# A vision block on one core: experts of the second image in swapped pairs, one write for the gates, and a new order on every engine

## What is computed

```python
# stage 1: gated 3x3 convolution (t = unfolded 3x3 patches, 576 values per pixel)
h1 = relu(t @ W1 + b1)
s = sigmoid(h1 @ W2 + b2)
h = (t * s) @ W3 + b3                      # 64 channels again; a class token is put in front
# stage 2: on n = layernorm(h)
a = n + linear_attention(rmsnorm(n, w_norm1)) @ w_out + b_out   # 8 heads, sums of k*v over all tokens of an image
h = h + a + rmsnorm(a, w_norm2)
# stage 3: on f = layernorm(h)
p = softmax(relu(f @ router_w1 + router_b1) @ router_w2 + router_b2)    # 6 experts
top_w, top_i = top_k(p, 2); g = softmax(top_w)
h = h + sum of g[k] * expert[top_i[k]](f)   # an expert is 64 -> 64 -> 64 -> 64 with relu; all six are computed
```

## Time and profile before

| | us |
|---|---|
| median of 3 runs | 2604.82 (2600.67 to 2604.88) |
| the profiled execution | 2603.84 |
| its span, first to last instruction | 2602.1 |
| TensorE busy | 2135.0 (82%) |
| VectorE busy | 1350.6 (52%) |
| ScalarE busy | 1103.6 (42%) |
| GpSimd busy | 511.4 (20%) |
| mean granted TensorE clock | 0.906 |

### The profile page before, as it was taken

The page is one execution under the profiler, slowest core; times in us unless marked ns, Lnnn a source line. Parts: engine busy times, 40 slices in busy tenths (PEclk is TensorE's granted clock), DMA queues, the critical chain, the costliest instruction groups (busy, mean ns, idle before and its releaser), DMA issues. The chain is left out here.

```text
span 2602.1 us, 36855 instructions
## 1 busy us (share of the span) xinstructions
PE 2135.0 (82%) x12353; PEld 921.4 (35%) x12353; DVE 1350.6 (52%) x3631; ACT 1103.6 (42%) x2213; POOL 511.4 (20%) x346
## 2 busy tenths in 40 slices
PE   7888878888878888888888888888888888876665
PEld 2333433333333333333334333333333333333322
DVE  4454646454545555564646464646464645544442
ACT  3443434444444444343534444444444444433233
POOL 1112212121221212122212121212121212121110
PEclk9998989899999989899989998999899999977777
DMA  2112222313131312222222222232313131211122
GB/s 106 61 61 63 63 71 53 84 46 91 46 91 46 88 49 80 57 69 68 69 68 67 71 66 71 57 81 56 81 46 91 46 91 46 51 43 43 44 48 58
DMA packets 41339, 168.30 MB, mean 65 GB/s; under 512 B 6048, under 2 KB 19264, under 8 KB 33984
## 3 DMA queue, kind: packets, MB, share of 16 engines
q1 hardware_dynamic: 41152, 165.95, 23.6%
HBM read 151.87 MB, written 14.05 MB: 64 GB/s over the span
## 5 line engine op out<-in xcount | busy, mean ns | idle before, releaser
L1243 DVE TENSOR_TENSOR gh<-f,gate_sp 128x448 f32<-128x448 f32 (+1 forms) x342 | 199.8, 612 | 436.5 <-issue 360.9
L682 ACT ACTIVATE th<-ps,b_half 128x448 f32<-128x448 f32 x504 | 294.8, 630 | 171.8 <-PE ps L354 106.4
L810 ACT ACTIVATE f<-ps,packed 128x448 f32<-128x448 f32 (+1 forms) x342 | 201.1, 630 | 371.9 <-DVE gh L1243 371.2
L920 DVE SCALAR_TENSOR_TENSOR gated<-th,x_tile 128x448 f32<-128x448 f32 x504 | 301.0, 617 | 16.3 <-PE ps L370 7.9
L388 PE MATMUL ps<-packed,rx_c 112*128 112x112 f32 (+1 forms) x225 | 56.7, 407 | 303.7 <-DVE rx_c L930 303.7
L856 POOL TENSOR_TENSOR rstd_u<-var_u,exponent 112x8 f32<-112x8 f32 (+1 forms) x57 | 92.3, 1619 | 1003.2 <-DVE var_u L946 1003.2
L326 PE MATMUL ps<-x_tile,packed 128*64 128x448 f32 x896 | 256.5, 693 | 2.0 <-DMA x_tile<-x_rows 2.0
L354 PE MATMUL ps<-h,packed 64*128 64x448 f32 x896 | 229.1, 588 | 9.8 <-ACT h L674 6.9
L370 PE MATMUL ps<-gated,w_half 128*64 128x448 f32 x896 | 203.7, 557 | 34.0 <-DVE gated L920 34.0
L856 POOL TENSOR_TENSOR rms_b<-ms_b,exponent 112x8 f32<-112x8 f32 (+1 forms) x57 | 107.3, 1882 | 591.2 <-DVE ms_b L1102 591.2
L610 PE MATMUL ps<-gh,packed 128*64 128x448 f32 (+1 forms) x684 | 216.7, 731 | 5.3 <-DVE gh L1243 5.3
(11 more groups left out here) (140 smaller groups left out, 3344.1 us busy)
## 6 DMA issues: line engine op xcount, KB each, us to landing
gate_sp<-gates_d SPq DMA_DIRECT2D x112, 672.0 KB, 7.0
x_tile<-x_rows SPq DMA_DIRECT2D x56, 696.0 KB, 5.2
x_tile<-x_rows SPq DMA_DIRECT2D x56, 580.0 KB, 3.8
out<-out_t SPq DMA_DIRECT2D x56, 224.0 KB, 8.1
gates_d<-gates_c SPq DMA_DIRECT2D x224, 5.2 KB
packed<-pack SPq DMA_DIRECT2D x1, 690.0 KB, 9.8
packed<-pack SPq DMA_DIRECT2D x1, 448.0 KB, 6.5
packed<-pack SPq DMA_DIRECT2D x1, 430.0 KB, 3.6
```

The source lines that it names most:

```text
L682: act.activation(th[(u + s) % 4][:, :], bank(S0 + u % 2), ACT.Tanh, bias=b2_half[:, m:m + 1], scale=0.5).then_inc(th_set, 1)
L810: act.activation(f2[j % 4][:, 0:n], bank(S0 + j % 2, n), ACT.Relu, bias=cst("eb2")[:, j:j + 1]).then_inc(f2_set, 1)
L920: dve.scalar_tensor_tensor(as_rows(gated[u % 4][:, :]), as_rows(th[(u + s) % 4][:, :]), 1.0, x_view(s, u), ALU.add, ALU.mult).then_inc(gat ...
L1243: dve.tensor_tensor(gh[j % 4][:, 0:n], f2[j % 4][:, 0:n], gate_sp[:, j, 0:n], ALU.mult).then_inc(gh_set, 1)
```

## The change

Image 1's experts are numbered with neighbours exchanged (1, 0, 3, 2, 5, 4) in the tables `rw2`, `order` and `eb3`. Its gates then come out of `gates_c` in an order in which even rows belong to the upper half and odd rows to the lower half for both images, so one write carries all 12 rows, and each read takes every second row. `gate_hidden` takes its slot accordingly. The order of the calls is new on every engine, and SyncE's list is longer by four steps.

```diff
-LAST_STEP = 70
+LAST_STEP = 74
@@ save_gates, spread_gates (SyncE)
-                for img in range(2):
-                    for low in range(2):
-                        top = (low + img) % 2
-                        sp.dma_start(gates_d[f % 2][top * E + img:top * E + E:2, 0:nt * tw],
-                                     gates_c[img * E + low:img * E + E:2, 0:nt * tw]).then_inc(gate_saved, 16)
+                sp.dma_start(gates_d[f % 2][:, 0:nt * tw], gates_c[:, 0:nt * tw]).then_inc(gate_saved, 16)
...
-                sp.wait_ge(gate_saved, 64 * f)
+                sp.wait_ge(gate_saved, 16 * f)
...
-                    rows = gates_d[f % 2][top * E:top * E + E, 0:n]
+                    rows = gates_d[f % 2][top:2 * E:2, 0:n]
@@ order on SyncE
-                if 1 <= step - 13 <= CLS_T: store_out(step - 13)
-                if 3 <= step + 1 <= BLOCKS: load_x(step + 1)
-                if 1 <= step - 10 <= CLS_T: save_gates(step - 10); spread_gates(step - 10)
+                if 3 <= step - 4 <= BLOCKS: load_x(step - 4)
+                if 1 <= step - 17 <= CLS_T: store_out(step - 17)
+                if 1 <= step - 14 <= CLS_T: spread_gates(step - 14)
+                if 1 <= step - 13 <= CLS_T: save_gates(step - 13)
@@ gate_hidden (VectorE)
-                dve.tensor_tensor(gh[j % 4][:, 0:n], f2[j % 4][:, 0:n], gate_sp[:, j, 0:n],
+                dve.tensor_tensor(gh[j % 4][:, 0:n], f2[j % 4][:, 0:n], gate_sp[:, j % 2 * (E // 2) + j // 2, 0:n],
@@ tables
+    swapped = [e + 1 - 2 * (e % 2) for e in range(E)]
+    for img, experts in enumerate((range(E), swapped)):
+        pack[img * E:img * E + E, eb3_at + 64 * img:eb3_at + 64 * img + 64] = eb3[list(experts)]
+        pack[RH * img:RH * img + RH, rw2_at + E * img:rw2_at + E * img + E] = a["L0_ffn_router_w2"][:, list(experts)]
+        pack[2 * RH, rw2_at + E * img:rw2_at + E * img + E] = a["L0_ffn_router_b2"][list(experts)]
...
+    put("order", np.tile(np.concatenate([first, first[swapped]]), (P, NT)))
```

More of the change, by code:

```diff
@@ L636, in _ @@
-                if 1 <= step - 1 <= BLOCKS: w3(step - 1, 4)
-                if 1 <= step - 9 <= CLS_T: spread_b(step - 9)
-                if 1 <= step - 10 <= CLS_T: gates_channels(step - 10); expert_h1(step - 10, 0)
+                if 1 <= step - 10 <= CLS_T: expert_h1(step - 10, 1); expert_h2(step - 10, 0)
+                if 1 <= step - 9 <= CLS_T: center_b(step - 9)
+                if 1 <= step - 10 <= CLS_T: expert_h1(step - 10, 2); expert_h2(step - 10, 1)
+                if 1 <= step - 9 <= CLS_T: var_mean_b(step - 9)
@@ L1309 @@
+                if 1 <= step - 8 <= CLS_T: spread_c(step - 8)
+                if 1 <= step - 9 <= CLS_T: gate_hidden(step - 9, 3)
 def kernel(**inputs):
```

139 lines of the change are left out of this document (65 added, 74 removed).

## The result

The change takes 2602.74 us (median of 4 runs, 2599.18 to 2604.88) to **2185.4 us** (4 runs, 2181.48 to 2196.58): a ratio of 0.8405, 95% interval 0.837 to 0.8439. The forecast was 2206 us in a range of 2170 to 2310. The profiled execution took 2188.09 us, its span is 2186.3 us.

A forecast was written before the change was run, and what follows sets the result against it. Bound: the 12.8 us gates-to-`gh` transfer, whose stall and slow clock cost 8.25 of 44.1 us a step. Middle 368, start 4 and end 27 give 399 us less: 2206 us, range 2170 to 2310.

The forecast's parts named there:

- Removed issues: SyncE's gate writes: one in place of four, 0.7 us an issue, about 2.1 us off the path from gates to reads.
- The walk through TensorE's queue: One step followed from `w2(0)`: 34.7 us of TensorE work at full clock, plus three gaps, giving 36.0 us.
- The slack of the gates' transfer: Reads' landing to `gh`: VectorE may idle 1 us; TensorE has no gap, with slack of about 1 us.
- First gap: TensorE at `w3(2)` waits for VectorE's `gate_pixels` 5, which end at 10.8 to 11.0: 0.6 us a step.
- Second gap: TensorE, done with `bias` and `h1(0)` at 17.8, waits for `spread_b`, ready at 18.1: 0.35 us a step.
- the second rival: TensorE's clock does not stay up over short gaps; one fall costs 2.75 us a step, 2330 us; chance 0.08.
- Third gap: `out_copy` waits for the store of two blocks before, taken as landed at 20.3: 0.4 us, ends 0 and 3.1.
- Fourth rival: Slower: strided reads behind x and store land so late that the stall grows; 50.7 us a step, 2910 us; chance 0.04.
- first rival: Store or reads come later than assumed, queued in one line: 1.8 us a step, 2289 us, up to 2330; chance 0.19.
- End of the program: After the last block the gates' loop bounds: 2.7 us less in each of 10 rounds, 27 us.
- Start: First nine steps, attention half alone: 20.5 us instead of 21, 8 x 0.5 = 4 us less.
- The third rival: Gates come no earlier as VectorE's new interleaving runs late; only 3.5 us a step gained, 2416 us; chance 0.07.

The follow-up runs named there:

- experiment 2: Changed kernel with four gate writes of every second row, as before, and contiguous reads, in the new order: 2258.42 us, 0.8664.
- experiment 3: Kernel before, old order on every engine, with only the single write, swapped expert pairs and strided reads: 2550.37 us, 0.9779.
- 4: Kernel before with the single write and swapped experts, plus SyncE's x load moved behind the gates' write and reads: 2442.99 us, 0.9368.
- experiment 11: Changed kernel with GpSimd's sum ahead of its power and the output store issued one step earlier: 2120.31 us, 0.8141.
- experiment 6: Changed kernel with SyncE's reads of the gates ahead of the x load and the store: 2623.16 us, 1.0057.
- 9: Changed kernel with the gates' transpose and copy later, behind the last `w3` and `unfold_out`, and the bias behind `expert_h2(0)`: 2382.63 us, 0.9137.
- experiment 5: Changed kernel with one write that sorts the rows into halves, and contiguous reads: 2188.39 us, 0.84.

## Why the prediction was right, and which of its terms were mis-sized

**Removed issues.** Said: 0.7 us each, 2.1 us off the path. The issues did shrink by 2.4 us (2.75 to 0.33), and in the new order that is worth 73 us (experiment 2). But the sum took them as if the write began with its issue. In the old order a single write is held by the x load ahead, and the same edit gives 0.67 us a step (experiment 3, and 4 for the cause); behind the last block, without that load, it gives 2.5 us a round, as the sum had it. I had not weighed this for the old order, where SyncE's queue showed the load 2.6 us ahead of the first write.

**The walk through TensorE's queue** held: 34.7 us of work a step; the version without stalls takes 34.9 (experiment 11). The other points of the walk, from `w2(0)` at 982.8 (0.73 us behind `hidden`, as 1058.02 and 1057.29 in the earlier trace rows):

| | forecast | measured |
|---|---|---|
| gates in SBUF | 13.2 | 12.7 |
| x load issued | 13.9 | 13.1 |
| store issued, landed | 15.0 to 15.6, 20.3 | 14.0, 19.8 |
| reads issued | 15.6 | 14.5 |
| first `gh` | 25.6 plus up to 1 | 26.4 |
| next `w2(0)` | 36.0 | 35.7 |

"Landed" is the start of `out_copy`, which waited for it. The slack of the gates' transfer, which is what the move was to buy, was sized rightly: `gh` waits 0.8 us, TensorE in these steps never for `rx_c`, and for `expert_out` 1.0 us in the whole run.

**First gap, 0.6 us: absent.** The step that failed is the length of VectorE's stretch: it was to take 9.4 us (its own terms add up to 9.5) and takes 8.0, so that pixels 5 end at 9.6, ahead of TensorE's 10.2. I priced `gs_dif` with its compare at 1.1 and `g_w` with its reduction at 0.8 us from the earlier trace rows; `gs_dif` and `g_w` themselves take 0.16 and 0.20 us. Those rows of before had caught both beside GpSimd's power and sum, and the new order takes them away from there.

**Second gap, 0.35 us: 1.03, and it took the clock with it.** The same step failed in the other direction: the copy `rx_b` was priced at 0.4 us and takes 1.34, since it now starts while GpSimd's sum runs. I had checked that GpSimd's own order was unchanged and so priced it at nothing; what it runs beside did change. In 11 of 46 steps the clock fell to half behind this gap for 3.6 us, about 1.6 us each, 17 us in all: the second rival, in small. I had ruled it out with "no gap over 1 us"; the gap was 1.03. The Trainium skill ("TensorE: Matmul & The Clock Gate", A second HAM failure mode: psum-queue depth-cycling) tells of a kernel whose clock goes up and down by short idles between groups of matmuls. The trace after agrees in that the clock fell behind an idle of 1.03 us, but its cause is one late copy in each step and not the use of PSUM, which no run here tests.

**Third gap, 0.4 us: nearly none.** The store landed at 5.7 us, between my bounds of 2.8 and 8.1, and was issued 1.0 to 1.6 us earlier than I put it. Over 1 us of wait on ScalarE stays hidden in most steps and shows in six, by 1.3 to 3.5 us of wait on TensorE. The rival priced this as an even 1.8 us in each step; in truth it is rare here. But what experiments 2, 6 and 9 lose, they lose mainly through it. **The store, which I treated as a term of 0.4 us, is the most sensitive place of the new order.** The reads, for which I walked the transfer so carefully, had room.

The three gaps were to be 1.35 us together and are 1.03, though none of the three is right by itself: that the even step came out at 35.67 where 36.0 was forecast is in part luck.

**Fourth rival.** Strided reads cost nothing (experiment 5). A slower kernel can be had from this order, but by the first rival's mechanism, which I had ended at 2330 us: with the store issued behind the reads it is at 1.0057 of before (experiment 6).

**End of the program.** Said -27, measured -69.4 us. From one `gates_copy` to the next, beside the earlier trace rows:

```profile
2044.84 0.53 ACT L788 ACTIVATE gates_c<-ps 12x448 f32<-12x448 f32 x1 [2.41 <-PE ps L546]
...
2072.11 0.53 ACT L788 ACTIVATE gates_c<-ps 12x448 f32<-12x448 f32 x1 [2.41 <-PE ps L546]
```

27.27 us against 33.32. By the timelines of both: write to reads -2.3 (I had 2.1), `gs_max` to `g_all` -3.0, `gh` to `gs_max` -1.8, the last vector operation to the copy -0.7, and reads to `gh` +1.8, since `gh` now stands behind `variance_b` on VectorE and starts with it, without a wait for the gates. The 3.0 were not in the sum. Of them 1.7 are small operations: in each round of before two of the gates', such as `g_o` and `g_w`, took 1.02 to 1.10 us beside GpSimd's power and sum, and all take 0.20 now. It is the mis-sizing of the first gap again, and here it lies on the path. The other 1.3 are the sum and scaling of the mean square and the copy `rx_b`, which stood ahead of `g_all` and now stand behind it.

**Start.** Said -4, measured +0.7: the fill steps take 20.71 us instead of 21.07, as nearly expected, but the step from block 9 to 10, the first with all stages, takes 35.3 us instead of 33.05.

The sum: -415.8 us of span against -399 said. The middle gave 21 us too little, the end 42 too much, the start 5 too little; the total is closer than its parts, and that is luck. The third rival's sum, 2602 - 161 - 27, is 2414 and not 2416 (2416 with the 1.7 us outside the span), which changes nothing.

## What to carry to other kernels

When an order is rewritten, price each short operation by what runs beside it in the new order, on the engine that it shares something with, and not by its old row: here a copy of 0.4 us became one of 1.3 us and cost 2% of the run, and one swapped pair of calls on GpSimd gave it back. Follow every transfer that is queued behind the one that the change is about, to its last consumer: not the reads of the gates but the output store, queued behind the write and the x load, was what a delay hit. And put a store where its buffer's next writer has a whole step, not where it happens to be ready.
